# A decoder layer with 32 experts: the tiles of the expert stage become (expert, block) pairs, added into blocks on chip and scattered to their places

## What is computed

```python
logits = xs @ router_w.T                       # 1024 x 32
scores = sigmoid(logits)
_, idx = top_k(scores + bias, 4)               # 4 of 32 experts per token
w = take_along_axis(scores, idx); w = w / (w.sum(-1) + 1e-20)
out = sum over experts e of (silu(xs @ wg[e]) * (xs @ wu[e])) @ wd[e] * combine[:, e]
out = out + (silu(xs @ sw_gate) * (xs @ sw_up)) @ sw_down
```

## Time and profile before

| What | us |
|---|---|
| Median of three runs (515.42 to 517.07) | 516.66 |
| The profiled execution | 515.59 |
| Its span | 513.8 |
| PE busy | 484.1 (94%) |
| DVE busy | 399.2 (78%) |
| ACT busy | 294.9 (57%) |
| POOL busy | 192.0 (37%) |
| PE's granted clock, mean of the span | 0.998 |

### The profile page before, as it was taken

How to read it: one execution, slowest core, us unless ns; L and a number is a source line. 1 busy time by engine, 2 the same in 40 slices (tenths; PEclk the granted TensorE clock), 3 DMA queues, 4 the chain that set the end, 5 groups by cost and what they waited for, 6 DMA issues and landing times.

```text
span 513.8 us, 11540 instructions
## 1 busy us (share of the span) xinstructions
PE 484.1 (94%) x3228; PEld 432.2 (84%) x3228; DVE 399.2 (78%) x1015; ACT 294.9 (57%) x831; POOL 192.0 (37%) x231
## 2 busy tenths in 40 slices
PE   6899999999999999999999999997998999999994
PEld 6678899899899899899899898876986778888883
DVE  6679998988998998988998988868878575344472
ACT  2566764765765765665665656565533666655550
POOL 3217531311411411411410403633702776515773
PEclk9999999999999999999999999999999999999999
DMA  6351310210210220220210099229995455745665
GB/s 186 102 139 43 87 49 1 80 54 0 80 52 0 68 65 0 65 68 0 61 41 0 0 357 328 94 87 304 306 294 171 133 178 167 234 140 155 178 192 173
DMA packets 63269, 60.77 MB, mean 118 GB/s; under 512 B 5552, under 2 KB 60544, under 8 KB 63104
## 3 DMA queue, kind: packets, MB, share of 16 engines
q1 hardware_dynamic: 59024, 49.64, 32.3%
q0 software_dynamic: 3936, 10.55, 7.7%
q10 hardware_dynamic: 272, 0.13, 0.1%
HBM read 47.82 MB, written 20.87 MB: 134 GB/s over the span
## 4 chain that ended last, share of the span: by engine, by line
PE 68%; DVE 14%; issue 5%; POOL 4%; ACT 4%; DMA 2%; POOLq 0%; DVEq 0%; SPq 0%; ACTq 0%
PE bank L987 14%; PE bank L989 13%; PE bank L988 13%; PE bank L1228 11%; PE bank L1236 5%; PE bank L1068 4%; DVE qk_lo L1723 3%; DVE rmax L1731 2%; PE bank L1362 1%; ACT qk_hi L1472 1%; PE bank L993 1%; ACT prob L1480 1%; PE bank L1232 1%; DVE nmax L1735 1%; POOL yg L888 1%
## 5 line engine op out<-in xcount | busy, mean ns | idle before, releaser
L1480 ACT ACTIVATE prob<-bank,nmax 128x256 f32<-128x256 f32 x128 | 59.6, 471 | 106.1 <-DVE nmax L1735 104.2
L697 POOL TENSOR_TENSOR w_lo<-st_c,w_hi 128x512 fp32r<-128x512 f32 x32 | 41.1, 1285 | 198.6 <-ACT w_hi L1443 198.6
L1228 PE MATMUL bank<-moe_w,xT 128*128 x252 | 65.4, 382 | 0.0
L1723 DVE SCALAR_TENSOR_TENSOR qk_lo<-bank,b_col,qk_hi 128x512 fp32r<-128x512 f32 x64 | 47.9, 748 | 15.5 <-ACT qk_hi L1472 14.7
L987 PE MATMUL bank<-hT_hi,w_lo 128*128 128x512 f32 x128 | 52.7, 412 | 5.7 <-DVE qk_lo L1723 3.0
L1731 DVE TENSOR_REDUCE rmax<-bank 128x2 f32<-128x512 f32 x64 | 43.9, 686 | 13.7 <-PE bank L989 13.2
L989 PE MATMUL bank<-hT_hi,w_hi 128*128 128x512 f32 x128 | 50.6, 395 | 0.0
L988 PE MATMUL bank<-hT_lo,w_hi 128*128 128x512 f32 x128 | 50.5, 394 | 0.0
L1228 PEld LDWEIGHTS bank<-moe_w,xT 128*128 128x128 f32 x252 | 45.3, 190 | 5.3
L1472 ACT ACTIVATE qk_hi<-bank,b_col 128x512 fp32r<-128x512 f32 x64 | 44.1, 688 | 7.3 <-PE bank L989 5.9
L1749 DVE TENSOR_SCALAR prob<-prob,rinv 128x256 f32<-128x256 f32 x128 | 46.4, 404 | 2.3
(11 more groups left out here) (270 smaller groups left out, 1473.4 us busy)
## 6 DMA issues: line engine op xcount, KB each, us to landing
y_dram<-ysb SPq DMA_DIRECT2D x63, 128.0 KB, 2.4
moe_w<-in_w_gate SPq DMA_DIRECT2D x8, 512.0 KB, 8.4
moe_w<-in_w_up SPq DMA_DIRECT2D x8, 512.0 KB, 7.7
moe_w<-in_w_down SPq DMA_DIRECT2D x4, 1024.0 KB, 9.0
st_c<-in_wq_codes SPq DMA_DIRECT2D x16, 128.0 KB
st_c<-in_wk_codes SPq DMA_DIRECT2D x16, 128.0 KB
st_c<-in_wv_codes SPq DMA_DIRECT2D x8, 256.0 KB
st_c<-in_wo_codes SPq DMA_DIRECT2D x8, 256.0 KB
```

The source lines that it names most:

```text
L1228: mm = pe.matmul(o, xT_of(kt), w, start=kt == 0, stop=kt == KT - 1)
L1480: ex = act.activation(prob[:, i % 4, qt, :], bS[i % 2][:, qt * S:(qt + 1) * S], ACT.Exp, bias=nmax[:, i % 2, qt:qt + 1], scale=SCALE, accu ...
L1723: dve.scalar_tensor_tensor(out=qk_lo[:, hp, m, n * HALF:(n + 1) * HALF], in0=src[:, :], scalar=b_col[:, bass.ds(g_h + m * H, 1)], in1=qk_h ...
```

## The change

**Tiles.** A tile is now a pair of an expert and a block of 128 sorted rows that holds rows of it. It is always read from the start of the block (`row_of` is a multiple of 128), so rows of other experts are computed too. `in_block` has a 1 for the rows of the tile's own expert and a 0 for the others. There are still 63 steps. To find the pairs, DVE works out first and last block of each expert (`first_i`, `first_f`, `tiles_e`, `low_e`, `count_e`), and from them, after the tables of before, `limits` and `upto` (seven more small instructions). PE spreads them over the partitions with three matmuls (`edges` on PE), and DVE makes `in_block` and `finished` (how many tiles each block needs) in step 0 (`edges` on DVE).

**Sums on chip.** ACT's copy to `ysb` and SP's 63 stores go. Instead DVE adds the down result of tile j-3 in step j, from PSUM, times its column of `in_block`, into its block of `y_rows` (`add_rows`). `y_rows` is 33 blocks of 1 KB per partition, laid over `x_in`, `h_row`, `pT_hi`, `pT_lo`, `prob` and `bo_b`; POOL clears blocks 0 to 7 and the spare one, ACT blocks 8 to 31 in steps 6 to 29 (`clear`). The 8 MB of copies of L614 go too, since no row is left unwritten now.

**Scatter.** Each finished block goes from `y_rows` with one indirect DMA from POOL to `y_dram`, which is now laid out as (rank, token): rank 0 to 3 is the order of a token's four slots. The table `send` of where each row goes is made like `source`: DVE works out the order of each token's slots (`ranks`, step 1) and `in_send` (step 2), PE does 32 more matmuls in step 4 (`destinations`, L1327's kind), DVE reads the result in step 5 (`send_rows`). `in_slot` is kept until then in the place of `h_row`. To have the token's own number, `x_all` carries it as column 256 through the scatter and back at 336 to 347 us, so those rows are 257 elements long.

**Loads.** The 32 gathers of L888 become 32 plain loads from SP, each when `y_done` has reached the blocks it needs.

**Beside the loop.** `extra_work` and `extra_sum` go, `gain_work` and `gain_sum` are in halves of 256 elements (steps 3 to 10), `add_shared` is one a step (11 to 18), and gain total, gain order, gain place, slot order and slots follow in steps 19 to 23 (twice eight small instructions `by_order`). So the table is stored to `x2_dram` after step 23. Sorting in trip 4 goes. Loads of registers on DVE are one step later each.

The diff, cut to its core:

```diff
@@ SyncE
-            spare = y_dram.rearrange("(n r) d -> n r d", r=T)
-            for n in range(TILES * SLOTS // T):
-                sp.dma_start(spare[n], a["x"].rearrange("b s d -> (b s) d")).then_inc(d_spare, 16)
...
-                    sp.dma_start(y_dram[bass.ds((it * STEPS + u) * SLOTS, SLOTS), :], ysb[:, u, :]).then_inc(d_y[u], 16)
...
+            sp.wait_ge(v_slot, S_TAB)
+            sp.wait_ge(v_sh, NT)
+            sp.dma_start(x2_dram.rearrange("(t p) d -> p t d", p=P), x_all[:, :, :]).then_inc(d_x2, 16)
...
+            for i, (t, n) in enumerate(load_order):
+                if i % NT == 0:
+                    sp.wait_ge(y_done, (n + 1) * NT)
...
+                sp.wait_ge(y_done, sp.snap(at[t], min_val=1, max_val=ROWS))
+                sp.dma_start(home(n)[:, t, :], places[column(n), t]).then_inc(d_yg[t][place_of(n)], 16)
@@ GpSimd
             scatter(1)
+            pool.memset(y_rows[:, 2:NT, :], 0.0).then_inc(p_zero, 1)
+            pool.memset(y_rows[:, ROWS, :], 0.0).then_inc(p_zero, 1)
             ln_root(pool, 1, 1)
...
-                pool.indirect_dma_start(out=home(k)[:, t, :], out_offset=None, in_=y_dram,
-                                        in_offset=bass.IndirectOffsetOnAxis(ap=y_slot[:, t, k:k + 1], axis=0)).then_inc(d_yg[t][place_of(k)], 16)
+            def landed(n):
+
+                pool.wait_ge(d_sc[n % STEPS], 16 * (n // STEPS + 1))
+                pool.sem_inc(y_done, 1)
+
+            for n in range(ROWS):
+                if n >= LAG:
+                    landed(n - LAG)
+                pool.wait_ge(t_gu, SH + min(USED, BESIDE + n * 15 // 16))
+                pool.wait_ge(v_add, pool.snap(at[n], min_val=1, max_val=TILES))
+                apart(pool)
+                pool.indirect_dma_start(out=y_dram, out_offset=bass.IndirectOffsetOnAxis(ap=send[:, n:n + 1], axis=0),
+                                        in_=y_rows[:, n, :], in_offset=None).then_inc(d_sc[n % STEPS], 16)
@@ TensorE
+            def destinations():
+
+                pe.wait_ge(v_val, 1)
+                for c in range(CH):
+                    mm = pe.matmul(send_at, in_slot[:, :, c], in_send[:, :, c], start=c == 0, stop=c == CH - 1)
+                mm.then_inc(t_r, 1)
...
-                        wait(pe, a_y, 0 if first and u < 4 else j - 3)
+                        wait(pe, v_add, 0 if first and u < 4 else j - 3)
                         down(u - 2 + STEPS, expert(j - 2))
+                    if j == SEND_AT:
+                        destinations()
@@ ScalarE
-                        act.copy(ysb[:, s, :], bY[u % 2][:, 0:D]).then_inc(a_y, 1)
+                    if isinstance(it, int) and NT <= j + 2 < ROWS:
...
+                        clear(j + 2)
@@ VectorE
+            def add_rows(j):
+                dve.wait_ge(t_dn, j + 1 + SH)
...
+                dve.scalar_tensor_tensor(out=here, in0=bY[j % 2][:, 0:D].rearrange("p (s a) -> p s a", s=SLOTS),
+                                         scalar=in_block[:, j:j + 1], in1=here, op0=ALU.mult, op1=ALU.add).then_inc(v_add, 1)
...
                         tile_copy(j + 1, u + 1, j + 2 if u < rows else ROWS)
+                    if j >= 3:
+                        add_rows(j - 3)
                     for work_beside in beside.get(u, ()):
...
+            aside = [edges, ranks, destinations]
+            aside += [lambda n=n: (gain_sum if n % 2 else gain_work)(*pairs[n // 2]) for n in range(2 * len(pairs))]
+            aside += [lambda t=t: add_shared(t) for t in range(NT)]
+            aside += [lambda: (gain_total(), gain_scale()), gain_order, gain_place, slot_order, slots]
```

More of the change, by code:

```diff
@@ L663, in _ @@
-            for it in range(ROW_TRIPS):
-                store(it)
-            with sp.Fori(ROW_TRIPS, TRIPS - 1) as it:
-                store(it)
-            store(TRIPS - 1, True)
-            for u in range(LAST - AFTER, LAST):
-                stored(u, TRIPS - 1)
+            sp.wait_ge(v_slot, S_TAB)
+            sp.wait_ge(v_sh, NT)
+            sp.dma_start(x2_dram.rearrange("(t p) d -> p t d", p=P), x_all[:, :, :]).then_inc(d_x2, 16)
+            at = [sp.alloc_register(f"need{t}") for t in range(NT)]
@@ L1657, in _, with clear @@
                 shared_copy(n)
+            def clear(b):
+                act.wait_ge(t_r, 8)
+                wait(act, v_sh, b - 3 * NT + 1)
+                act.copy(y_rows[:, b, :], y_rows[:, ROWS, :]).then_inc(a_zero, 1)
             def trip(it, first, last, rows=0):
                 steps = LAST if last else STEPS
-                for u in range(steps + (2 if last else 0)):
+                for u in range(steps + (1 if last else 0)):
                     j = it * STEPS + u
@@ L2032, in tile_copy, with edges @@
                                 xT_all[:, :, bass.ds(row_of_tile(j), SLOTS)]).then_inc(v_x, 1)
-            def gain_work(half):
+            def edges():
+                dve.wait_ge(t_r, 7)
+                own(dve.memset(xT_all[:, :, ROWS * SLOTS:(ROWS + 1) * SLOTS], 0.0))
+                own(dve.tensor_scalar(below[:, :], edges_at[:, 0:TILES], tile_no[:, 0:1], None, ALU.is_le))
+                own(dve.scalar_tensor_tensor(out=in_block[:, :], in0=edges_at[:, TILES:2 * TILES], scalar=tile_no[:, 0:1],
+                                             in1=below[:, :], op0=ALU.is_gt, op1=ALU.mult))
+                dve.tensor_copy(finished[:, :], edges_at[0:1, 2 * TILES:2 * TILES + ROWS]).then_inc(v_send, 1)
@@ new lines, in destinations, with send_rows, by_order @@
+            def destinations():
+                dve.tensor_tensor(in_send[:, :, :], in_tile[:, :, :], send_id[:, :].unsqueeze(1).to_broadcast([P, ROWS, CH]),
+                                  ALU.mult).then_inc(v_val, 1)
+            def send_rows():
+                dve.wait_ge(t_r, 8)
+                dve.tensor_scalar(send[:, :], send_at, float(T * TOPK // 2), None,
+                                  ALU.add).then_inc(v_send, 1)
+            def by_order(values):
+                for half in range(2):
+                    hs = slice(half * HT, (half + 1) * HT)
+                    for r in range(TOPK):
+                        ins = dve.scalar_tensor_tensor(out=pairwise[:, r, hs, :], in0=order[:, half, :, :].rearrange("p k t -> p t k"),
+                                                       scalar=float(r), in1=values(half), op0=ALU.is_equal, op1=ALU.mult)
+                own(ins)
```

345 lines of the change are left out of this document (187 added, 158 removed).

## The result

The changed kernel takes **521.69 us** (median of four runs, 521.44 to 522.03) against 516.85 for the kernel before, measured beside it: ratio 1.0107, 95% interval 1.0087 to 1.0127. It is slower by 4.8 us. The forecast was 518.7 with a range of 516.0 to 523.5, and "slower" had 0.60.

A forecast was written before the change was run, and what follows sets the result against it. PE was taken to set the pace, bar 1.3 and 0.55 us of loop stalls. Terms 0.1 + 0.4 + 2.2 - 0.7 + 0.3 - 0.25 + 0.4 - 0.25 = +2.2 us gave 517.8 profiled, 518.7 as median, range 516.0 to 523.5.

The forecast's parts named there:

- the prediction's own signs of being wrong: Loop and tail: steps 3 to 18 above 1.8 us, combining stage waiting for SP's loads, or loop end before 499.5.
- `destinations`: Step 4 on PE: 32 matmuls for the send table, hidden by nothing, +2.2 us, bounds 1.8 and 2.5.
- the router stage: Ahead of the loop: extra small DVE instructions delay PE, `edges` matmuls fit in its wait; +0.4 us, bounds 0 and +1.
- Spare copies and stores: 300 to 321 us: removing 8 MB copies, 63 stores and ACT's 63 copies gives 0, bounds -0.9 and 0.
- Rows of 257 elements: Scatter and reload at 340 to 347 us: longer, unevenly starting rows cost +0.1 us, bounds 0 and +1.
- `add_rows` and DVE's pace: Tile loop: with DVE's adds, about 0.6 us of stall in place of 1.3, -0.7 us, bounds -1.3 and +3.
- rival 3: Trips 0 to 3: DVE sets the pace, each add 0.15 us dearer, 2.5 us more behind, 521 us; chance 0.10.
- Table, sorting, last trip: Later loop: table gathers stall PE +0.3 us, sorting gone -0.25, last trip's diagonals and adds +0.4.
- Tail: After the loop: PE's products stay, last output issued at 509.25 where it was 509.5, -0.25 us.
- rival 2: Tail: the scatter train ends last at 1.45 us per scatter, its last starting at 504.5, 521 us; chance 0.08.
- 4: Scatter train: DVE's SBUF reads slow POOL's issue by 0.2 us per scatter, 522 us; chance 0.08.

The follow-up runs named there:

- experiment 3: Changed kernel with the eight spare copies (8 MB) put back: median 521.04 us, ratio 1.0087 against the kernel before.
- send_twice: Changed kernel with the 32 matmuls of the send table issued twice: median 526.38 us, ratio 1.0187 against the kernel before.
- after_copies: Changed kernel with the eight spare copies put back, the same run as experiment 3: median 521.04 us, ratio 1.0087.
- experiment 7: Changed kernel with DVE's ten register loads for tiles 24 and up moved to steps 22 to 58, run twice: 0.9992 and 0.9954 against before, on other chips.
- control_before: The kernel before, unchanged, run and profiled once more: ratio 0.9998, profile 516.24 us.
- rows257: The kernel before with only its sorted table's rows lengthened to 257 elements: median 516.89 us against 516.56, ratio 1.0005.
- experiment 1: The kernel before, unchanged, run once more, the same run as control_before: ratio 0.9998, profile 516.24 us.
- experiment 2: The kernel before with only its sorted table's rows lengthened to 257 elements, the same run as rows257: median 516.89 us, ratio 1.0005.
- placed_as_after: The kernel before with the attention's buffers at the changed kernel's SBUF places, no instruction changed: ratio 1.0016, where the kernel before takes 544.21 us.

## Why the prediction was right, and where its sum was off

The sign, the range and the largest term were right, but the forecast of 518.7 was 3.0 us short: the sum reached +2.2 where the medians differ by 4.8 and the profiled executions by 6.2. Two of the prediction's own signs of being wrong came in part: four of the steps 3 to 18 took over 1.8 us without a table in them, and the combining stage waited for SP's loads. That the range held is luck in part: it was made wide enough for the rivals on DVE and on the train, which had 0.10 and 0.08, and these are what came, beside 0.8 us from a stage that the sum does not mention. "Slower" itself did not need luck: `destinations` and the router stage, the terms that were argued, give 3.2 us in the measured lengths. Step by step:

- **Spare copies and stores, 0.** Right for the copies, by experiment 3. Nothing in the table speaks against 0 for the stores, but no run puts them back.
- **Rows of 257 elements, +0.1, bounds 0 and +1.** Right within its bounds: +0.3 us in the runs, with landings 0.6 and 0.2 us longer, mostly before `source` and in part hidden. Why 257-element rows land later is not shown.
- **Router stage, +0.4.** 1.27 in the profile. In send_twice, which had the higher clock there, it was 402.27 - 395.09 = 7.18 for 6.36, +0.8; the rest is the stretch at 1.2 GHz, when the matmuls of two shared products took 1.50 and 1.41 us for 1.03. (The 8.28 of after_copies has a late gather in it.) DVE gave PE its `row_of` 0.55 us later behind `source`, where 0.45 was counted. The error is PE's: the `edges` matmuls were to take 0.3 us and to fit into its wait of 0.41 for the second gather. That wait was gone, since PE was late already, and they took 0.73 us of PE's path.
- **`destinations`, +2.2, bounds 1.8 and 2.5.** Right: 2.39, and 2.37 for the second pass. It is bare, that is, nothing hides it, also with DVE late behind it. 0.4 us more came in step 2, where DVE's work on the edges made it 2.09 us for 1.73; the prediction had no term for it.
- **`add_rows` and DVE's pace, -0.7.** This is the step that failed, and by the sign. The sum had 1.3 us of old stall fall to 0.6 (its own terms, 4 x 0.07 and 0.5, make 0.8); it became 2.84 (43.59 - 25 x 1.63). The mis-sized number is DVE's need in a step. With a register load 1.15 us was counted (0.21 + 0.45 + 0.20 + 0.29), and it is 0.29 + 0.40 + 0.29 + 0.29 = 1.27; a gain half beside it was counted at 0.55 and takes 0.62 to 0.64. So such a step needs 1.9 us, not 1.70, and PE's 1.63 is missed by 0.27 and not by 0.07. The first of these errors could be seen in the earlier trace rows: there 0.58 us pass from the product to the copy with a load between them, and the count has 0.20 + 0.29. The loads of 0.29 us in steps 8 to 12 did not fit beside the halved gains, and so all of the old stall stayed (1.30 us in steps 6 to 13). Moving them took 0.2 us off steps 10 and 11, on other chips (experiment 7). The steps with `add_shared`, counted at 1.60, did fit from step 14 on: that piece takes 0.33 us and not 0.45. Steps 20, 21 and 23 added 1.57, where 1.0 less 0.5 of slack was counted. The stall beyond the forecast, 2.2 us, is close to the 2.5 that rival 3 has for a DVE that sets the pace. Its mechanism is another, though: it had each add cost 0.15 us more, and copy and add together take 0.69 us where 0.66 was counted.
- **Table, sorting, last trip: +0.45 together.** Measured +0.19. Step 34 waited as predicted (0.9 us for the gather, 0.35 to PE), the last trip's diagonals cost nothing: its steps are 1.41 to 1.46 us, not 1.5.
- **Tail, -0.25.** Two errors against each other, -1.3 us together. PE waited 1.3 us for the last rank, 0.92 of it in the end: rival 2's mechanism. The last scatter was to start at 497 to 502, and started at 506.48; the loop's end itself was 5 us later than forecast. It was to decide from 502.1 on, 3.9 us behind the forecast's `gate_up` 62 (495.74 + 2.45); measured, it decides at 3.17 us behind and not at 1.86. That part differs between executions: PE's chain from `gate_up` 62 on is 11.89 us in the changed kernel, 10.99 in after_copies and 13.16 in send_twice. Against it stand 2.23 us between PE's end and the span's, where 0.25 was counted. Half a microsecond is that DVE's last add comes sooner behind PE. For the rest, 4.34 us from the last output's issue to the span's end have become 2.62. In before the last indirect DMA is issued 3.7 us ahead of the last output, now 11.0. That the end of before waits for GpSimd's queue has support in three traces: the span ends 8.0 us behind the start of the last gather in before, control_before and rows257 alike (505.79, 506.47 and 511.30), while it ends 4.34, 4.10 and 3.62 us behind the issue of the last output. No run was made to try it. The prediction took the last output for the end of the program and so had no term for it.
- **Not in the sum at all: +0.8 us in the attention stage**, from the places of buffers, and some 0.2 us of the 4.8 from the clock (experiment 1). The prediction looked at the layout only for races and reuse.

Of the rivals, 4 did not come: the 32 scatters took 0.97 to 1.05 us. The rule that it took from the Trainium skill (SBUF — State Buffer, "SBUF: two separate sides") names the fp32 copy within SBUF as an operation that keeps GpSimd from writing descriptors, so it speaks of the tile copies and not of the adds, which read PSUM. It is not seen in the loop after the change either: the 23 scatters that overlap a tile copy took 0.98 us on average, the nine others 0.97. Nor in before, where the prediction's "all others took 0.95" leaves out the gathers from `h_dram`: they take 1.01 us on average beside a tile copy and 1.03 without one.

What made the rival think of it is real, however. In before the gather of 1.67 us beside the twelve adds of the combining stage ends 0.82 us behind the last of these adds (502.97 and 502.15). In control_before it is again 1.67 us and ends 0.82 us behind them, and in rows257 one of 3.24 us does so (507.25 and 506.43, the two rows in experiment 2). Others ran beside the same adds in 0.95 us, and what tells the two kinds apart is not shown. These adds have both operands in SBUF and follow each other without a gap; those of the loop have one in PSUM and come once a step. In the changed kernel no indirect DMA is left to wait for them.

## What to carry to other kernels

Count an engine's need in a step from copy to copy of a step in which it is the late one, and put every register load in that sum. A count that comes within 0.07 us of the pace decides nothing when its terms are off by 0.1 each. When work is moved from a queue to the engine that comes second, spread the loads and small instructions of that engine before adding to it; here that took 0.2 us off a step, and what it does to the whole time was not measured. When buffers change places, compare the stretch in which nothing else changed: it is the cheapest control that a trace has. And look for what the end of the program waits for: it need not be the last output.

## What the hardware showed that was not expected

- The same instructions on buffers at other places in SBUF ran 0.3% slower over 290 us of attention (0.84 to 0.93 us in 291). PE's products of `pT_lo` and then `pT_hi` start 118 ns apart where it was 117, which is a small part of it.
- One program took 517 us on one chip and 544 on two others. Up to 340 us they agree within 1 us. Most of the rest comes in the tile loop: 119.3 us from `gate_up` 0 to 62 in placed_as_after, which has before's instructions, and 95.2 in control_before, so 24 of 26.5 us. It comes in waits of 1.5 to 4 us on PE, DVE and ACT that the profile puts down to no instruction or DMA of this core.
- The granted clock fell to 1.2 GHz for stretches of 3.4 us and of 6.8 (once 13.7), in either kernel and not in every run, after PE had idled or had worked on 32-column matmuls; whether it happened, and behind which of these, changed between kernels that were the same up to there.
- On the first chip the end of before lies 8.0 us behind the start of the last indirect DMA on GpSimd in three traces, whatever the last output does.
- Eight scalar_tensor_tensor of 128x16 elements took 0.77 to 0.85 us together: they start about 0.1 us apart, each 0.16 to 0.18 us long.
